# Attention maps in pairs of sides on four row groups, with the key tile's work cut into bursts

## The reference, cut to what matters

```python
DIM, H, HD = 128, 16, 4                     # 16 heads, two "sides" of 4 channels each
qkv = x @ w_qkv.T                           # x: 2 x 1024 x 128
q = q.reshape(B, N, H, 2, HD); k = k.reshape(B, N, H, 2, HD); v = v.reshape(B, N, H, 2 * HD)
def sdpa(qi, ki):
    p = softmax(einsum('bnhd,bmhd->bhnm', qi, ki) * HD ** -0.5, axis=-1)
    return einsum('bhnm,bmhe->bhne', p, v)
a1 = sdpa(q[:, :, :, 0], k[:, :, :, 0]); a2 = sdpa(q[:, :, :, 1], k[:, :, :, 1])
o = rms_norm(a1 - lam * a2) * 0.8           # per head, over 8 channels
return o.transpose(0, 2, 1, 3).reshape(B, N, C) @ w_proj.T + b_proj
```

## Time and profile before

| | us |
|---|---|
| time, median of 3 runs | 3686.81 (3684.1 to 3694.66) |
| the profiled execution's own time | 3684.8 |
| its span | 3683.0 |
| `attention_maps`, first matmul (89.15) to last copy (1109.42) | 1020.3 |
| `join_maps`, first transfer issued (1114.28) to the next stage's first matmul (1200.72) | 86.4 |

### The profile page before, as it was taken

The page is one execution under the profiler, slowest core; times in us unless marked ns, Lnnn a source line. Parts: engine busy times, 40 slices in busy tenths (PEclk is TensorE's granted clock), DMA queues, the critical chain, the costliest instruction groups (busy, mean ns, idle before and its releaser), DMA issues. The chain is left out here.

```text
span 3683.0 us, 71336 instructions
## 1 busy us (share of the span) xinstructions
PE 3280.8 (89%) x25164; PEld 1821.2 (49%) x25164; DVE 2741.0 (74%) x3715; ACT 2013.3 (55%) x2780; POOL 1119.2 (30%) x709
## 2 busy tenths in 40 slices
PE   4999999999995688888888888888889888869997
PEld 2222222222224455556555565656555565548886
DVE  2777777777753598979888797989898887946664
ACT  2455555555551366666667676766666676621111
POOL 2000000000001464645455454555464454610000
PEclk7899999999995799999999999999999999979999
DMA  3000000000002210011011001001110110100001
GB/s 114 11 16 15 14 15 15 15 15 15 15 14 93 66 29 24 29 48 34 18 35 48 24 29 54 29 24 29 53 29 23 29 35 21 32 23 1 0 0 29
DMA packets 70710, 107.05 MB, mean 29 GB/s; under 512 B 26790, under 2 KB 41012, under 8 KB 69684
## 3 DMA queue, kind: packets, MB, share of 16 engines
q1 hardware_dynamic: 69716, 104.37, 9.8%
q10 hardware_dynamic: 864, 0.79, 0.1%
HBM read 38.79 MB, written 15.73 MB: 15 GB/s over the span
## 5 line engine op out<-in xcount | busy, mean ns | idle before, releaser
L924 DVE TENSOR_REDUCE a_part_max<-a_ps_max 128x1 f32<-128x512 f32 x1024 | 683.2, 691 | 290.6 <-PE a_ps_max L846 288.7
L822 ACT ACTIVATE a_expT<-a_ps_scoresT 128x1024 f32<-128x1024 f32 x512 | 517.0, 1024 | 314.6 <-PE a_ps_scoresT L858 309.2
L1614 DVE STREAM_TRANSPOSE b_probsT<-b_probs 32x1024 f32<-32x1024 f32 x384 | 474.3, 1235 | 94.3 <-POOL b_probs L1240 85.2
L867 PE MATMUL a_ps_out<-a_expT,a_v_op 128*32 128x512 f32 x2048 | 537.6, 605 | 0.7 <-issue 0.5
L1216 POOL TENSOR_TENSOR b_turned_q<-b_rot_q,b_turned_q 128x1024 f32<-128x1024 f32 x96 | 226.8, 2363 | 711.3 <-DVE b_turned_q L1548 711.3
L846 PE MATMUL a_ps_max<-a_k_op,a_q_op 96*128 96x512 bf16 x1024 | 401.3, 392 | 25.7 <-DMA a_k_op<-terms_k 21.8
L846 PEld LDWEIGHTS a_ps_max<-a_k_op,a_q_op 96*128 96x128 bf16 x1024 | 98.3, 96 | 516.2 <-DVE a_part_max L924 428.6
L1441 PE MATMUL b_psD<-b_probsT,b_v 128*64 128x128 f32 x3072 | 337.8, 278 | 5.8 <-DVE b_probsT L1614 5.8
L1442 PE MATMUL b_psD<-b_probsT,b_v_back 128*64 128x128 f32 x3072 | 332.8, 274 | 0.0
L1456 PE MATMUL b_psD<-b_w_qkv,b_xs 128*128 (+1 forms) x384 | 211.3, 638 | 111.6 <-ACT b_outT L1305 111.6
L858 PE MATMUL a_ps_scoresT<-a_q_op,a_k_op 128*128 128x512 bf16 x1024 | 306.8, 380 | 0.0
(11 more groups left out here) (294 smaller groups left out, 5907.9 us busy)
## 6 DMA issues: line engine op xcount, KB each, us to landing
b_v_back<-b_v SPq DMA_DIRECT2D x96, 384.0 KB, 3.5
b_v_back<-b_v SPq DMA_DIRECT2D x96, 128.0 KB, 3.4
b_w_qkv<-L_ffn_Wqkv SPq DMA_DIRECT2D x6, 1536.0 KB
sums<-a_outT SPq DMA_DIRECT2D x512, 16.0 KB
j_got<-sums SPq DMA_DIRECT2D x16, 512.0 KB
a_q_op<-terms_q SPq DMA_DIRECT2D x64, 48.0 KB
a_k_op<-terms_k SPq DMA_DIRECT2D x64, 48.0 KB
b_w_o<-L_ffn_Wo SPq DMA_DIRECT2D x6, 512.0 KB
```

What stands on the lines that cost most here:

```text
L822: act.activation(expT[kt % RING][:], ps_scoresT[kt % 2][:], ACT.Exp, scale=SCALE_A).then_inc(exp_ready, 1)
L867: last_mm = pe.matmul(ps_out[lo:lo + 32, :], v_op[(u // 2) % 2][:, kt, :], expT[kt % RING][:, 512 * half:512 * half + 512], start=(kt < 2) ...
L924: dve.tensor_reduce(part_max[:, qt, half:half + 1], ps_max[half][:], AX.X, ALU.max).then_inc(max_taken, 1)
L1614: dve.transpose(probsT[rows, :, :, rows].rearrange("p c h q -> p h c q"), probs[rows]).then_inc(probsT_ready, 1)
```

## The change

Two maps, the two sides of one head, are worked on together; `p` is such a pair (32 of them). The array's 128 rows are used as four groups of 32: `group(side, copy)` is 32 x (2 x side + copy). Each side's 24 rows of terms are loaded twice, into two groups, and each group has its own two rows for the maximum and its own ones.

- PE's step for key tile kt of pair p: the maximum's scores of unit u (one query tile of one side: two matmuls of 512 keys in two row groups, to one `ps_max` of 1024 columns); two score matmuls of side 1 in the other two row groups; `weigh` part 0; then unit u+1 (the other side), two score matmuls of side 0, `weigh` part 1. A part is four matmuls of 256 queries, one to each of four column groups (two sides, two halves).
- The scores of a pair are numbered n = 32p + 4kt + ..., and go to one `ps_scoresT` of three buffers of 512, by n mod 3. ACT takes two of them (1024 columns), then one (512), and so on, into a ring of 18 places. Score n waits for the exponential of n-3.
- DVE reduces all 1024 columns of a unit at once, negated, into one column of `minus_max`, so the two partial maxima and L927, L931, L933 are gone. Per pair PE turns 16 columns (fp32) into `ps_row`, which lies in `ps_max[1]`; DVE makes the two bf16 parts (`row_out`), ACT's copy L799 is gone; SP sends 8 rows. The turn stands behind the first unit of the next pair but in the order of PE; the second unit waits for `max_lo_ready`.
- The outputs of a pair go by 8 transfers from `outT` straight to SBUF (`joined`); `sums`, its reads, and the adds L524 and L532 are gone. `v_aug` is 32 wide and is used without the copy to `v_op`.
- POOL sets `k_op` to one (4 memsets, 128 rows), SP starts pair 0's loads after the first of them. The four-map loops are written out straight.

```diff
-            def max_scores_of(turn, slot, qt, first=False, halves=(0, 1)):
-                ...
-                    pe.matmul(ps_max[half][:], q_op[slot][0:ROW, P * qt:P * qt + P], k_op[slot][0:ROW, 512 * half:512 * half + 512],
-                              start=True, stop=True).then_inc(max_scores, 1)
+            def max_scores_of(u):
+                p, qt, side = u // UNITS, u % UNITS // 2, u % 2
+                ...
+                if u >= 2:
+                    pe.wait_ge(max_taken, u - 1)
+                if u % UNITS == 1 and p >= 1:
+                    pe.wait_ge(max_lo_ready, p)
                 for half in range(2):
+                    lo = group(side, half)
+                    last_mm = pe.matmul(ps_max[u % 2][:, 512 * half:512 * half + 512], q_op[slot][lo:lo + ROWS, P * qt:P * qt + P],
+                                        k_op[slot][lo:lo + ROWS, 512 * half:512 * half + 512], start=True, stop=True)
+                last_mm.then_inc(max_scores, 1)
+                if u % UNITS == 0 and p >= 1:
+                    turn_row(p - 1)
+            def turn_row(p):
+                pe.wait_ge(max_taken, UNITS * (p + 1))
+                pe.transpose(ps_row, minus_max[p % 2][:], ident[:]).then_inc(row_turned, 1)
+            def scores(p, kt, side, place):
+                ...
+                for half in range(2):
+                    n = HALVES * p + 4 * kt + place + half
+                    lo = group(side, half)
+                    if n >= 3:
+                        pe.wait_ge(exp_ready, exp_of(n - 3) + 1)
+                    pe.matmul(ps_scoresT[:, 512 * (n % 3):512 * (n % 3) + 512], k_op[slot][lo:lo + ROWS + 2, P * kt:P * kt + P],
+                              q_op[slot][lo:lo + ROWS + 2, 512 * half:512 * half + 512], start=True, stop=True).then_inc(scoresT_ready, 1)
+            def weigh(p, kt, part):
+                ...
+                for place, (side, half) in enumerate(((1, 0), (1, 1), (0, 0), (0, 1))):
+                    lo = group(side, half)
+                    at = 512 * ((n + place) % SLOTS) + 256 * part
+                    last_mm = pe.matmul(ps_out[lo:lo + 32, 256 * part:256 * part + 256], v_aug[:, b * T8 + kt, head, :], expT[:, at:at + 256],
+                                        start=(kt == 0 and part == 0), stop=(kt == T8 - 1), skip_group_check=True)
+            for u in range(UNITS + LEAD):
+                max_scores_of(u)
+            for p in range(PAIRS_A):
+                pe.wait_ge(row_in[p % RING], 128 * (p // RING + 1))
+                for kt in range(T8):
+                    u = UNITS * (p + 1) + LEAD + 2 * kt
+                    ...
+                        max_scores_of(u)
+                    scores(p, kt, 1, 0)
+                    if kt >= 2:
+                        weigh(p, kt - 2, 0)
+                    ...
+                        max_scores_of(u + 1)
+                    scores(p, kt, 0, 2)
+                    if kt >= 2:
+                        weigh(p, kt - 2, 1)
```

```diff
+        @block.vector
+            def row_out(p):
+                dve.wait_ge(row_turned, p + 1)
+                ...
+                dve.tensor_copy(max_hi[p % 2][:], ps_row).then_inc(max_hi_ready, 1)
+                dve.wait_ge(max_hi_ready, p + 1)
+                dve.tensor_tensor(max_lo[p % 2][:], ps_row, max_hi[p % 2][:], ALU.subtract).then_inc(max_lo_ready, 1)
+            for u in range(UNITS * PAIRS_A):
+                ...
+                dve.tensor_reduce(minus_max[p % 2][:, at:at + 1], ps_max[u % 2][:], AX.X, ALU.max, negate=True).then_inc(max_taken, 1)
+                if u % UNITS == 0 and p >= 1:
+                    row_out(p - 1)
+        @block.scalar
+            for e in range(EXPS):
+                first = 3 * (e // 2) + 2 * (e % 2)
+                size = min(2 - e % 2, HALVES * PAIRS_A - first)
+                ...
+                act.activation(expT[:, to:to + 512 * size], ps_scoresT[:, at:at + 512 * size], ACT.Exp, scale=SCALE_A).then_inc(exp_ready, 1)
+                if end >= HALVES * (copied + 1) + 8:
+                    out_copy(copied)
+                    copied += 1
+        @block.sync
+            def rows(p):
+                slot = p % RING
+                sp.wait_ge(max_hi_ready, p + 1)
+                sp.wait_ge(max_lo_ready, p + 1)
+                for side in range(2):
+                    for copy in range(2):
+                        lo = group(side, copy) + ROWS
+                        sp.dma_start(q_op[slot][lo:lo + 1, :], max_hi[p % 2][T8 * side:T8 * side + T8, :]).then_inc(row_in[slot], 16)
+                        sp.dma_start(q_op[slot][lo + 1:lo + 2, :], max_lo[p % 2][T8 * side:T8 * side + T8, :]).then_inc(row_in[slot], 16)
```

More of the change, by code:

```diff
@@ L711, in attention_maps, with group @@
         out_sent = [sem(f"out_sent{i}") for i in range(2)]
-        T8 = TILES_PER_BATCH
+        def group(side, copy):
+            return 32 * (2 * side + copy)
         block = ctx.enter_context(nc.Block())
@@ L740, in _ @@
-            for M in range(3):
-                operands(M, M)
-            row(0, 0, 0)
-            def step(M, u, more, first=False):
-                if not first:
-                    sp.wait_ge(pv_done, T8 * M)
-                if more:
-                    operands(M + 3, (u + 3) % RING)
-                row(M + 1, (u + 1) % RING, (u + 1) % 2)
-                if not first:
-                    store(M - 1, (u + 1) % 2)
-            for u in range(RING):
-                step(u, u, True, u == 0)
@@ L756, in _ @@
-            with sp.Fori(1, MAPS // RING - 1) as turn:
-                for u in range(RING):
-                    step(RING * turn + u, u, True)
-            for u in range(RING - 1):
-                step(MAPS - RING + u, u, u == 0)
-            store(MAPS - 2, 0)
-            store(MAPS - 1, 1)
+                            lo = group(side, half) + VD_A * kind
+                            sp.dma_start(joined[b][at:at + VD_A, kind, side, 512 * half:512 * half + 512],
+                                         outT[p % 2][lo:lo + VD_A, :]).then_inc(out_sent[p % 2], 16)
@@ new lines, in _ @@
+            for p in range(RING - 1):
+                sp.wait_ge(ones_set, p + 1)
+                operands(p)
+            rows(0)
+            for p in range(PAIRS_A):
+                if p == 0:
+                    sp.wait_ge(ones_set, RING)
+                else:
+                    sp.wait_ge(pv_done, T8 * p)
+                if p + RING - 1 < PAIRS_A:
+                    operands(p + RING - 1)
+                if p >= 1:
+                    store(p - 1)
+                if p + 1 < PAIRS_A:
+                    rows(p + 1)
@@ L824, in _, with out_copy @@
-            for u in range(RING):
-                step(0, u, first=(u == 0))
-            with act.Fori(1, MAPS // RING - 1) as turn:
-                for u in range(RING):
-                    step(turn, u)
-            for u in range(RING):
-                step(MAPS // RING - 1, u, last=(u == RING - 1))
-            act.wait_ge(out_sent[1], 128 * (MAPS // 2 - 1))
-            out_copy(MAPS - 1, 1)
+            def out_copy(p):
+                act.wait_ge(pv_done, T8 * (p + 1))
+                if p >= 2:
+                    act.wait_ge(out_sent[p % 2], 128 * (p // 2))
+                act.activation(outT[p % 2][:], ps_out[:], ACT.Copy).then_inc(out_held, 1)
@@ L862, in weigh @@
-            def weigh(M, u, kt):
-                pe.wait_ge(exp_ready, T8 * M + kt + 1)
-                for half in range(2):
-                    lo = 32 * (2 * (kt % 2) + half)
-                    last_mm = pe.matmul(ps_out[lo:lo + 32, :], v_op[(u // 2) % 2][:, kt, :], expT[kt % RING][:, 512 * half:512 * half + 512],
-                                        start=(kt < 2), stop=(kt >= T8 - 2))
-                last_mm.then_inc(pv_done, 1)
-            for qt in range(T8):
-                max_scores_of(0, 0, qt, True)
```

267 lines of the change are left out of this document (84 added, 183 removed).

## The result

The changed kernel takes **3574.55 us** (median of 4 executions, 3569.4 to 3584.42), the kernel before, run beside it, 3685.45 (3680.57 to 3694.66). The ratio is 0.970, 95% interval 0.967 to 0.973: 111 us faster, where 257 were forecast. The profiled execution took 3573.86 us, its span is 3572.0; against the 3683.0 of before that is 111.0 less, and it goes as follows.

What follows compares the result with a forecast made beforehand. PE was taken to bound the kernel before, the ACT-PE buffer exchange the changed one. 3684.8 - 233 (stage) - 8 (start) - 18 (join) = 3426 us profiled, median 3428; range 3365 to 3590.

Steps and rivals of the forecast that it cites:

- The clock: PE in `attention_maps`: no gap longer than some 1.5 us, so the full clock (2.4 GHz) was kept.
- the clock stays low: Rival: PE stays at 1.2 GHz after the first maxima; 3570 to 3635 us, part of the time low 3500; chance 0.14.
- The terms of the sum: `attention_maps`: 29 us ahead, 32 pairs at 23.6, 3 behind; 787 us against 1020, -233.
- Half step: PE's burst 0.30, turn 0.10, weighing part 0.43, turn back 0.13: 0.96 us, against a tile step of 1.955.
- The exchange: ACT and PE waiting for each other over three score buffers: 8.0 us per three key tiles, 21.4 per pair; the new bound.
- Row groups in turn: Rival: a burst's four matmuls run one after another, 0.853 us, half step 1.51; kernel 3482 us; chance 0.14.
- Slower: Rival: low clock and each turn waits for a matmul's tail, 0.34 per turn; kernel 3750 us; chance 0.06.
- Better, DVE is the bound: Rival: turns or ACT's latency shrink, stage 688 us; kernel 3327, half way 3375; chance 0.12 for 3330 to 3380.
- DVE's floor: DVE in `attention_maps`: 1.215 us per reduction of 1024 columns, about 20.5 per pair, 656 for 32.
- At the seam: Between two pairs: ACT's copy 0.5, maxima's turn 0.4, second unit 0.5, rows landing 0.8; together 2.2 us per pair.
- The join: After the stage: reads and adds go, 11.2 and 1.23 us, and some 6 more from later adds; -18 us.
- The setting: Before the stage: the first load waits for one memset instead of 12 and two more; -8 us.

Runs made afterwards that it cites:

- experiment 6: The changed kernel with one extra bf16 matmul of 128 rows and 512 columns ahead of each of the first 38 units only; 3562.72 us.
- Experiment 3: The changed kernel with burst matmuls over all 128 rows but 128 of 512 columns, three quarters of the scores left out; 3363.64 us.

## Why the prediction was wrong, point by point

- **The step that failed is "The clock"**: "The forecast has no gap longer than some 1.5 us, so I keep the full clock". Two things were wrong in it. It took an idle gap as the only thing that lowers the clock; the earlier trace rows had already shown 0.50 in the lead-in for PE working in pieces, so there was no full clock to keep: it had to rise first. The runs show that with 24 and 26 rows in the bursts the clock stays at 0.50 with PE 97% busy, and that 28 or 32 rows bring 0.89 to 0.94 (the setting that goes with them does nothing alone). And the seam's wait is 1.73 us, not 1.5: all four falls with 24 and 26 rows while maxima are made, one in the change and three in experiment 6, came during that wait or within 2.3 us of its end. Why the rows matter stays open.
- **The rival "the clock stays low" had the right size and too small a chance.** It gave 10.1 us per three key tiles, 28 to 30 per pair, 930 to 995 for the stage and 3570 to 3635. Measured: 5.07 per three half steps (maxima at 508.18 and 513.25), so 10.1 per three key tiles; 28.4; 927; 3574.55. What I set against it, "at 1.2 GHz PE itself would be nearly without gaps, as where the clock rose at 116", was the error: PE is without gaps, and the clock doesn't rise. The page "TensorE: Matmul & The Clock Gate" of the Trainium skill, Part 1 (What's actually happening), says that the default state is throttled and activity releases the throttle. The traces don't agree if activity is read as time at work: 194.70 of 200 us at 0.50, against 166.55 of 200 at 0.96 with 32 rows.
- **The terms of the sum** hold at the full clock. Half step 0.90 for 0.96; the burst with its turn is 0.33 where I had 0.30 + 0.10. The exchange: maxima at 378.13, 382.09 and 386.05, 3.96 per three half steps, 7.92 per three key tiles, forecast 8.0. The pair 23.3, forecast 23.6. The lead-in took 27.2 (82.89 to 110.13), forecast 29. With 32 rows the stage is 766.6 us (80.92 to 847.54) against 787, mostly by 22.9 per pair instead of 23.6, and the kernel 3410.69 against 3428.
- **Row groups in turn** fell: they start together. **Slower** fell: the turns at 1.2 GHz cost 0.11 and 0.17 (0.54 - 0.427 and 1.02 - 0.853), not 0.34. The page "TensorEngine Tiling (Array Packing)" of the Trainium skill, Key Properties, says that a change of tiling mode drains TensorE. My estimate from it, the whole tail of 0.17 at the full clock, isn't reached: a turn costs 0.12 and 0.14 (0.33 - 0.213, 0.57 - 0.427), near the 0.10 and 0.14 of before. **Better, DVE is the bound**: not reached; even with 32 rows PE's scores wait 61.2 us in all for ACT. DVE's floor is lower than I had it, too: in the lead-in its reductions start 1.13 us apart (83.54 to 84.68 and so on), not 1.215.
- **Experiment 3, at 21.4 per pair, comes nearest**, and not mainly by its clock. Where a score has waited for ACT, it streams 128 columns instead of 512, and the weighing can follow sooner. First the version with 32 rows, then experiment 3:

```profile
351.88 0.39 PE L797 MATMUL a_ps_scoresT<-a_q_op,a_k_op 32*128 32x512 bf16 x1 [0.25 <-ACT a_expT L758]
352.19 0.64 PE L811 MATMUL a_ps_out<-a_expT,v_aug 128*32 128x256 f32 x8
```
```profile
312.25 0.23 PE L797 MATMUL a_ps_scoresT<-a_q_op,a_k_op 128*128 128x128 bf16 x1 [0.28 <-ACT a_expT L758]
312.41 0.64 PE L811 MATMUL a_ps_out<-a_expT,v_aug 128*32 128x256 f32 x8
```

  0.31 against 0.16 us. Three half steps take 3.99 (maxima at 357.52 and 361.51) against 3.59 (310.29 and 313.88), which is 2.1 per pair; 0.5 of it goes back into longer waits for the rows at the seams (26.2 us in all in experiment 3, 10.5 with 32 rows).
- **At the seam** the rows cost less than the 0.8 that I took each time: with 32 rows PE waits 1.8 us for them ahead of the first pair and 8.7 in 13 of the other 31 cases, 0.3 per pair. In the change's slow stretches they are in time. The turn's wait for DVE is 0.2 per pair (forecast 0.4); ACT's copy and the second unit cost more, 0.9 and 0.7 (forecast 0.5 and 0.5). These waits add up to some 2.0 where I had 2.2, which is luck, as none of the parts was right. Waits of the 32-row version (engine, what, line, released by: us in total, times, longest; 80 to 848 us):

```profile
PE a_ps_scoresT L797 <- ACT a_expT L758: 61.2, 232, 0.8
...
PE a_ps_out L811 <- ACT a_outT L747: 27.7, 31, 1.7
...
PE a_ps_max L778 <- DVE a_max_lo L851: 20.3, 29, 1.3
...
PE a_ps_max L778 <- DMA a_q_op<-a_max_lo: 10.5, 14, 1.8
PE a_ps_max L787 <- DVE a_minus_max L859: 5.2, 13, 0.4
```

- **The join** gained 12.4, not 18. From the end of the last copy to the join's first matmul 17.3 us became 7.7 (1009.64 to 1017.34), a gain of 9.6 where the rows gave 12.4: the 8 outputs to SBUF took 5.29 us to issue (from 1009.66), the 8 to HBM before 2.65 (from 1109.45). The "some 6 more" was a guess; the rest of the join gained 2.7. **The setting** gained 6.3, not 8.
- **SP** was said to issue "14 us of transfers per 23.6", but the prices given, 8 x 0.38 + 8 x 0.33 + 5.6, make 11.3. It is 14 by luck: with 32 rows 8 loads took 3.2 us, 8 outputs 5.35 and 8 rows 5.4 (343.77 to 360.41, with a wait in between). The outputs cost twice the price that I took.

## What to carry to other kernels

Before packing a matmul of few rows into row groups, ask what it does to the clock: the packing saves streaming time, but here the stage lost the full clock by it, and with it 140 of the 233 us that it was to gain. If a stage shows a granted clock of 0.50 with PE busy throughout, try first to fill the unused rows of the groups with zeros (it adds no column and no matmul), and only then think of extra matmuls. Read every price at both clocks, and give "the clock is low" the chance that the nearest row of the trace gives it, not the one that a busy engine suggests.

## What the runs showed of the hardware that was not expected

- The number of rows that the matmuls of this stage use changes their speed through the clock: 24 and 26 rows in four groups 0.50, 28 rows 0.89, 32 rows 0.94, with the same instructions and columns, zero rows included. How the chip weighs rows, columns and time isn't settled by these runs.
- The clock has a memory in this stage: with 24 and 26 rows it held at 1.00 for up to two pairs and fell at the next wait of 1.7 us. It falls at that wait with 32 rows and with extra matmuls as well; what differs is how soon it is back, 3 to 14 us with 32 rows against mostly 300 us and more. What raised it near 349 us in the change, with nothing different in the program, stays open.
- More work made the kernel faster: 512 additional matmuls gave 80 us, of half the length 115.
